# Cross-attention and quantised FFN, one core: every per-group stage placed anew, and the second quantisation's scale read from PSUM

## What is computed

```python
def act_quant(x):
    scale = 127.0 / jnp.clip(jnp.max(jnp.abs(x), axis=-1, keepdims=True), 1e-05)
    return jnp.clip(jnp.round(x * scale), -128, 127) / scale
...
q_in = x @ Wq + _lora(x, q_down, q_up, q_alpha)
k_in = org_ctx @ Wk + _lora(org_ctx, k_down, k_up, k_alpha)
v_in = org_ctx @ Wv + _lora(org_ctx, v_down, v_up, v_alpha)
out = _attention(q_in, k_in, v_in)
out_ipa = _attention(q_in, ipa_ctx @ Wk_ipa, ipa_ctx @ Wv_ipa)
out = out + IPA_SCALE * out_ipa
return out @ Wo + bo + _lora(out, o_down, o_up, o_alpha)
...
h = bit_linear(x, w1)
h = depthwise_conv1d(h.transpose(0, 2, 1), conv_w, conv_b)
h = h.transpose(0, 2, 1)
h = jax.nn.silu(h)
return bit_linear(h, w2)
...
x = x + _L0_xattn_ref(_layernorm(x, axis=-1), ctx_768, ...)
x = x + _L0_ffn_ref(_layernorm(x, axis=-1), ...)
```

## Time and profile before

| | us |
|---|---|
| median of 3 runs | 1633.49 (1632.47 to 1634.84) |
| profiled execution | 1633.91 |
| its span | 1631.8 |
| PE busy | 1458.5 (89%) |
| DVE busy | 1244.0 (76%) |
| ACT busy | 1188.6 (73%) |
| POOL busy | 730.8 (45%) |

### The profile page before, as it was taken

One profiled execution on the slowest core, in us unless ns is written; L12 is line 12 of the kernel. 1 busy time (PEld: TensorE's weight loads), 2 busy tenths in 40 slices (PEclk: granted clock), 3 DMA queues, 4 the chain that ended last, 5 costly groups with the idle time before them and its releaser, 6 DMA issues.

```text
span 1631.8 us, 33414 instructions
## 1 busy us (share of the span) xinstructions
PE 1458.5 (89%) x10732; PEld 1190.0 (73%) x10778; DVE 1244.0 (76%) x3029; ACT 1188.6 (73%) x3925; POOL 730.8 (45%) x1085
## 2 busy tenths in 40 slices
PE   7999998999999999999999899999989999998742
PEld 3778787777777777777787777777877777776521
DVE  4263697887878788777879878786888878786876
ACT  2477886968778686968778696877869687886721
POOL 0144444554544444554444445454454445445510
PEclk9999999999999999999999999999999999999965
DMA  7300101000000100000010100001010000000000
GB/s 192 119 29 15 30 15 43 2 27 28 27 28 14 41 14 28 14 27 28 14 41 14 34 7 27 28 19 35 14 41 13 28 14 27 28 1 27 1 14 13
DMA packets 41129, 47.14 MB, mean 29 GB/s; under 512 B 3008, under 2 KB 35200, under 8 KB 41088
## 3 DMA queue, kind: packets, MB, share of 16 engines
q1 hardware_dynamic: 40032, 45.82, 9.1%
q10 hardware_dynamic: 1056, 0.81, 0.2%
HBM read 36.13 MB, written 10.49 MB: 29 GB/s over the span
## 4 chain that ended last, share of the span: by engine, by line
PE 32%; issue 29%; POOL 17%; DVE 13%; ACT 8%; DMA 0%; POOLq 0%; DVEq 0%; ACTq 0%
POOL SM L1033 8%; PE PS L462 6%; POOL OTl L1065 5%; PE PS L424 5%; PE PS L523 4%; ACT SM L650 3%; PE PS L475 3%; PE PS L449 3%; PE PS L405 3%; PE PS L440 3%; POOL XRES L1072 2%; PE PS L414 2%; DVE GBS L869 1%; DVE HP L754 1%; PE PS L542 1%
## 5 line engine op out<-in xcount | busy, mean ns | idle before, releaser
L1033 POOL TENSOR_TENSOR SM<-SM,RC 128x496 f32<-128x496 f32 (+1 forms) x512 | 338.9, 683 | 673.8 <-DVE RC L804 673.8
L650 ACT ACTIVATE SM<-PS,MX 128x124 f32<-128x124 f32 x1024 | 359.2, 366 | 160.1 <-DVE SM L810 158.0
L462 PE MATMUL PS<-KT,QM 128*128 128x128 f32 x2048 | 279.3, 280 | 25.6 <-ACT SM L650 25.4
L462 PEld LDWEIGHTS PS<-KT,QM 128*128 128x128 f32 x2048 | 251.4, 193 | 37.9 <-ACT SM L650 37.2
L1065 POOL TENSOR_TENSOR OTl<-OF,OTh 128x256 fp32r<-128x256 f32 x256 | 210.4, 822 | 16.0 <-ACT OF L644 15.2
L650 ACT ACTIVATION_READ_ACCUMULATOR SM<-PS,MX 128x1 f32 x1024 | 211.3, 206 | 0.0
L449 PE MATMUL PS<-IDF,SM 128*128 128x128 f32 x1024 | 168.4, 287 | 35.6 <-POOL SM L1033 35.4
L642 ACT ACTIVATE OTh<-PS 128x256 fp32r<-128x256 f32 x256 | 100.2, 392 | 113.1 <-PE PS L440 111.8
L808 DVE TENSOR_REDUCE MX<-PS 128x4 f32<-128x496 f32 x256 | 170.0, 664 | 0.0
L440 PE MATMUL PS<-PT,V 128*64 128x128 f32 x2048 | 169.2, 286 | 0.0
L449 PEld LDWEIGHTS PS<-IDF,SM 128*128 128x128 f32 x1024 | 107.8, 141 | 81.8 <-POOL SM L1033 43.8
(11 more groups left out here) (140 smaller groups left out, 3663.0 us busy)
## 6 DMA issues: line engine op xcount, KB each, us to landing
XIN<-in_x SPq DMA_DIRECT2D x16, 512.0 KB, 3.5
XRES<-in_x SPq DMA_DIRECT2D x16, 512.0 KB, 3.5
out_y<-HP SPq DMA_DIRECT2D x16, 512.0 KB, 3.0
CRAW<-in_ctxT SPq DMA_DIRECT2D x16, 256.0 KB, 2.7
RRAW<-in_ctxT SPq DMA_DIRECT2D x32, 128.0 KB, 2.9
QM<-in_Wq SPq DMA_DIRECT2D x1, 1024.0 KB, 10.8
GBS<-in_Wo SPq DMA_DIRECT2D x1, 1024.0 KB, 21.7
k_ipa_columns<-HP SPq DMA_DIRECT2D x1, 1024.0 KB, 5.1
```

The lines of the kernel that those rows point to most:

```text
L462: m = mm(psS[:, h, :], QM[:, 2 * q + h // 2, h % 2, TOK * b:TOK * b + TOK], KT[:, 2 * q + h // 2, b, :], start=True, stop=True)
L650: m = act.activation(SM[s % 2][:, h, 0:ORG], psS[:, h, 0:ORG], ACT.Exp, bias=MX[s % 2][:, h:h + 1], accum_out=SU[s % 2][:, h:h + 1])
L1033: m = pool.tensor_tensor(part, part, RC[c % 2][:, 4 * i:4 * i + 4].unsqueeze(2).broadcast_to(shape), ALU.mult)
```

## The change

**All places are new.** The units of a quad now come in the order Q K Q K V V, with a list of halves for each quad instead of a common pattern. The hidden tiles take the offsets 0, 1, 3, 4, 6, 7, 9, 10 instead of 0, 1, 2, 4, 5, 6, 8, 9, so everything behind them starts a half later, and the transposes of the maxima and the second broadcast come closer behind the maxima: M_HMAX 28 to 29, M_HT 30 to 31, M_BC2 32 as before, M_Q2 33 as before. The two blocks of the second product move from 36 and 38 to 38 and 40. The two residual sums move from halves 4 and 7 to 6 and 7, the largest absolute value gets a half of its own (10) and the scales half 11. The split of the context is in half 7 on ScalarE and 8 on VectorE, ScalarE's copies of the transposed input in half 9 instead of 8. The context's DMAs are issued at half 5 instead of 7, those of the image tokens' values at the halves of the first V.

**Second quantisation.** VectorE multiplies all eight tiles, and reads the scale from psF in PSUM; the copy to BC on ScalarE and the two multiplies on GpSimd are gone. Four tiles are done in half 33, two in 34, two in 35 (Q2_PLACE); the rounding is the same.

**Buffers.** XN2 and Q1 lie in GBS instead of HP. **GpSimd** issues the chunk's attention work ahead of the other stages in each half.

```diff
-U_Q, U_K, U_V = (0, 3), (1, 4), (2, 5)
+U_Q, U_K, U_V = (0, 2), (1, 3), (4, 5)
...
-N_CIN = 7
-N_CSPLIT = 8
+N_CIN = 5
+N_CSPLIT = (7, 8)
 N_KI = 10
-N_Q, N_K, N_V = (10, 14), (11, 15), (13, 16)
-N_QUAD = (0, 8, 15, 23)
+N_Q = ((10, 17, 24, 31), (12, 20, 27, 34))
+N_K = ((11, 18, 26, 33), (13, 21, 28, 35))
+N_V = ((15, 22, 29, 36), (16, 23, 30, 37))
...
-M_X2 = (4, 7)
+M_X2 = (6, 7)
 M_STATS = 7
-M_POW, M_NORM = 9, 9
-M_QT, M_BC1 = 13, 14
+M_POW, M_NORM = 8, 9
+M_ABS, M_SCALE = 10, 11
+M_QT, M_BC1 = 12, 14
 M_F1 = 15
-M_TILE = (0, 1, 2, 4, 5, 6, 8, 9)
+M_TILE = (0, 1, 3, 4, 6, 7, 9, 10)
...
-M_HT, M_BC2 = M_HMAX + 2, M_HMAX + 4
-M_Q2 = M_HMAX + 5
-M_F2 = (M_HMAX + 8, M_HMAX + 10)
+M_HT, M_BC2 = M_HMAX + 2, M_HMAX + 3
+M_Q2 = M_HMAX + 4
+M_F2 = (M_HMAX + 9, M_HMAX + 11)
 M_COPY = M_Q2 + 2
-Q2_DVE = CT - CT // 4
+Q2_PLACE = (0, 0, 1, 2)
...
-        XN2 = h_rows[:, 6:8, :].rearrange("p a (b d) -> p (a b) d", d=DM)
-        Q1 = h_rows[:, 5, :].bitcast(BF16).rearrange("p (b d) -> p b d", d=DM)
+        gb_flat = GBS[:].rearrange("p i b t -> p (i b t)")
+        XN2 = gb_flat[:, 2 * T:4 * T].rearrange("p (b d) -> p b d", d=DM)
+        Q1 = gb_flat[:, T:2 * T].bitcast(BF16).rearrange("p (b d) -> p b d", d=DM)
...
-                if n == N_XT:
+                if n == N_XT + 1:
                     for k in range(2):
                         act.wait_ge(unit_full, g.count(UNITS, k + 1))
...
-                for j in range(CT):
-                    if n == M_Q2 + j // 4 and j % 4 < 3:
-                        dve.wait_ge(bc_done, g.count(2, 2))
-                        if j >= 4:
-                            dve.wait_ge(q2_done, g.count(CT, j - 3))
-                        dve.tensor_tensor(GB[j % 4].rearrange("p b t -> p (b t)"), HT[j], BC[:], ALU.mult).then_inc(q2_scaled[0], 1)
...
+                pairs = [k for k in range(CT // 2) if n == M_Q2 + Q2_PLACE[k]]
+                for j in (2 * k + i for k in pairs for i in range(2)):
+                    dve.wait_ge(bc_full, g.count(2, 2))
+                    if j >= 4:
+                        dve.wait_ge(q2_done, g.count(CT, j - 3))
+                    dve.tensor_tensor(GB[j % 4].rearrange("p b t -> p (b t)"), HT[j], psF, ALU.mult).then_inc(q2_scaled, 1)
...
             def steps(g, n):
+                attend(g, n)
+                attend_low(g, n)
                 if g.exists():
                     project(g, n + HALVES)
...
                 residual(g, n)
-                attend(g, n)
-                attend_low(g, n)
```

More of the change, by code:

```diff
@@ L255, in program @@
         hm_done, ht_full = sem("hm_done"), sem("ht_full")
-        q2_scaled = [sem(f"q2_scaled{i}") for i in range(2)]
+        q2_scaled = sem("q2_scaled")
         q2_done = sem("q2_done")
@@ L884, in finish @@
                     scales(g, 1, 2 * CLIP, 127.0, 1.0 / 254.0)
-                for j in range(CT):
-                    if n == M_Q2 + j // 4 and j % 4 < 3:
-                        dve.wait_ge(bc_done, g.count(2, 2))
-                        if j >= 4:
-                            dve.wait_ge(q2_done, g.count(CT, j - 3))
-                        dve.tensor_tensor(GB[j % 4].rearrange("p b t -> p (b t)"), HT[j], BC[:], ALU.mult).then_inc(q2_scaled[0], 1)
-                for j in range(CT):
-                    if n == M_Q2 + j // 4:
-                        if j % 4 == 0:
-                            dve.wait_ge(q2_scaled[0], g.count(Q2_DVE, 3 * (j // 4) + 2))
-                        if j % 4 == 2:
-                            dve.wait_ge(q2_scaled[0], g.count(Q2_DVE, 3 * (j // 4) + 3))
-                            dve.wait_ge(q2_scaled[1], g.count(CT - Q2_DVE, j // 4 + 1))
+                pairs = [k for k in range(CT // 2) if n == M_Q2 + Q2_PLACE[k]]
[4 more added lines that the diff above has]
+                    dve.tensor_tensor(GB[j % 4].rearrange("p b t -> p (b t)"), HT[j], psF, ALU.mult).then_inc(q2_scaled, 1)
+                for k in pairs:
+                    dve.wait_ge(q2_scaled, g.count(CT, 2 * k + 2))
+                    for j in range(2 * k, 2 * k + 2):
                         dve.tensor_scalar(Q2[j], GB[j % 4].rearrange("p b t -> p (b t)"), MAGIC, MAGIC,
@@ L1039, in finish @@
                     pool.tensor_tensor(RS[1][:], VE[1][:], HALF[:], ALU.pow).then_inc(ln2_rstd, 1)
-                for j in range(CT):
-                    if n == M_Q2 + j // 4 and j % 4 == 3:
-                        pool.wait_ge(bc_done, g.count(2, 2))
-                        if j >= 4:
-                            pool.wait_ge(q2_done, g.count(CT, j - 3))
-                        pool.tensor_tensor(GB[j % 4].rearrange("p b t -> p (b t)"), HT[j], BC[:], ALU.mult).then_inc(q2_scaled[1], 1)
             for n in range(EARLY_HALVES):
@@ L1068, in residual @@
             def residual(g, n):
-                if n in (16, 18, 20, 22) and g.exists():
-                    b = (n - 16) // 2
+                if n in (17, 19, 21, 23) and g.exists():
+                    b = (n - 17) // 2
                     pool.wait_ge(xres_in, g.count(16, 16))
```

50 lines of the change are left out of this document (23 added, 27 removed).

## The result

The changed kernel takes 1590.87 us (median of four runs, 1588.63 to 1592.11), the kernel before beside it 1633.92: a ratio of 0.9736, interval 0.9719 to 0.9753. The profiled execution took 1588.63, its span is 1586.8.

The account below looks back on a forecast made before the run. TensorE was taken as the bound, gaining only from its waits and clock. Loop -35, groups 0 and 1 +4, group 15 -6 and drain -6 give -43 us, so 1633.9 becomes 1591; range 1552 to 1626.

Parts of the forecast that it names:

- The quantisation: Second quantisation: 0.68 us a multiply, 7.6 on VectorE; the 3.1 us of waits in chunk 1 and the low clock go.
- What is late next: Six TensorE waits per loop period that the new order makes or keeps, sum 4.9 us, 4.6 after a deduction.
- the second block: Second product, half 8: TensorE waits 1.5 us for VectorE's sum of the first block, behind chunk 4's maxima.
- the tiles: Two pairs of hidden tiles in consecutive halves of one chunk wait for VectorE's multiply, 0.8 and 0.7 us a period.
- TensorE's work: TensorE's busy time in a loop period: the same matmuls are issued, so 86.4 us stays.
- Rival (c): Loop: waits only move, sum stays 6.3, clock still falls, period 93.7; 1626 us, or about 1631 without group 15's gain; 0.12.
- The start: Groups 0 and 1: 4 us more, from a Q unit ahead of the first scores (1.4) and group 1's new waits.
- Group 15: The last group before the drain: 7 us less in chunks 0 to 4, 1 more behind, so 6 less.
- The drain: The chain at the end: quantisations, BC copy and a filled VectorE wait save, tiles cost 1.2; together 6 us less.
- (a): Loop: VectorE comes on time, small delays do not add up, only 1.8 us of waits; period 88.3, 1556 us; chance 0.18.
- (b): Second quantisation becomes the bound, multiplies 1.17 us from start to start; period 94.9, 1651 us; 0.08 with lesser forms.
- (d): The main forecast, but the clock falls every second period after the 1.5 us wait: 10 more, 1601 us; 0.62 together.

Follow-up runs that it names:

- r3: The changed kernel with the second scale copied to BC and all eight multiplies on VectorE reading it from there; 1614.0 us.
- r4: The changed kernel with VectorE's sum of the second product's first block one half earlier; 1595.1 us.
- r7: r1 with ScalarE's two copies of the transposed input one half later, behind that chunk's exponentials; 1582.9 us.
- r1: The kernel before with only the quantisation from PSUM, all eight multiplies on VectorE, four tiles in each of two halves; 1584.5 us.
- r6: The changed kernel with the projection's units, and the context's transfers and split, in the order and halves of before; 1566.2 us.
- r5: The changed kernel with all its new places but the old second quantisation (copy to BC, two multiplies on GpSimd); 1629.1 us.

## Why the prediction was right, point by point

**The total** was 1591 and came out at 1590.9, and that is partly luck. The loop gave 43.3 instead of 35, the drain 2.2 instead of 6, and the start cost 6.7 instead of 4 (2.3 of it the first scores, which scatter by as much); by the spans it is 45.0 less, where the sum had 43.

**The quantisation** was right in every number: 0.68 a multiply, 0.60 from start to start, 3.8 for the first piece (884.29 to 888.0), no wait for GpSimd's probabilities, no low clock. That the 65 ns more for an operand in PSUM would not show held too. What the text left open is which part of it matters. r3 shows it in part: the wait for the copy is the most of it, and the operand's place matters by what GpSimd's work beside it no longer does, not by a price of its own.

**What is late next.** All six terms came, each in its place: 1.2 for the second block (predicted 1.5), 0.6 for the maxima (0.8), 0.6 for the K copy (0.4), 0.5 for BC (0.7; some 0.3 without the matmul that the trace lacks), 0.8 and 0.8 for the tiles (0.8 and 0.7). Their sum is 4.6, as predicted after the deduction. But they are not six independent costs: r4 shows that the second block's 1.2 can go and the period stay, since chunks 5 and 7 then wait for GpSimd and for BC.

**TensorE's work** was to stay 86.4. It is 85.8: the mis-sized term. The prediction had the better number at hand: its list of the sixteen chunks adds up to 85.3, which the sum did not use. The loop's 43.3 are 24 for the waits (13 x (6.45 - 4.6)), 9.3 for the clock (6 x 1.55) and 9 for less work (13 x 0.7), where the sum of 35 has none for the last. Scores behind a wait for the exponentials read 1.16 where others read 1.06 (r7's row above). Measured to the next instruction's start, the scores of r1 take 0.91 behind such a wait and 0.81 otherwise, in four chunks (1, 4, 5, 13) of each period; the transposes ahead of the wait take 0.65 to their end, and 0.49 to the next start where nothing waits. They are not slower: the four start within 0.38 in both cases, but the last one's end, which otherwise lies under the first scores, stands alone ahead of a wait, and the first scores behind it are 0.10 longer. In the changed kernel all sixteen chunks have 0.81 and 0.49. Such a wait therefore costs some 0.26 more than its idle time, 1.0 a period; the rest of the period takes 0.3 more than in r1, which stays unexplained. r6 has 86.5 again, so the smaller work belongs to the units' new halves, whose idle time more than takes it back.

**The reason for the gain** was half wrong. I read the light and heavy chunks as the place "where the order loses". r1 has them all and the same period as after; r5, without them but with the old quantisation, has 93.1. The imbalance made a late engine visible, it was not the cause, and the new halves of the units, taken alone, lose 1.2 a period (r6). Rival (c), that waits only move, was right for the places, though not for the kernel.

**The start** was to cost 4. Groups 0 and 1 cost 4.4 between them. The 1.4 for a Q unit ahead of the first scores cannot be seen in the scatter there; group 1, with 3.4, costs more than I gave it. r6 has both back.

**Group 15** was to give 6 and gave 6.1, by 6.3 in chunks 0 to 4 and 0.2 lost behind, where the prediction had 7 and 1.

**The drain** was to give 6 and gave 2.2. The two quantisations gave 2.4 and 0.8 (10.2 to 7.8 and 8.6 to 7.8 us from first multiply to last rounding), as predicted together. The copy to BC gave 0.6 in the last group (2.97 to 2.34 us from the last scale to the first multiply), not 0.8; filling VectorE's 3.1 us wait gave 0.65, not 2.4, since the second block runs at the lower clock level there and makes VectorE wait 2.39 itself (its 16 matmuls take 3.58 at a granted clock of 0.52; before they took 1.92 at 1.00). The prediction's sum for the drain has no term for the clock:

```profile
1520.13 0.88 DVE L818 SCALAR_TENSOR_TENSOR HP<-PS,AD,HP 128x256 f32<-128x256 f32 x2 [0.51 <-PE PS L525]
...
1524.68 0.88 DVE L818 SCALAR_TENSOR_TENSOR HP<-PS,AD,HP 128x256 f32<-128x256 f32 x2 [2.39 <-PE PS L525]
```

The tiles cost 0.1, not 1.2. And a term was missing: the maxima stand a half later, so from the last scores to the first multiply it is 10.05 instead of 7.76, 2.3 more.

**Small sums.** 4.4 + 1.6 + 0.8 is 6.8, not 6.9, and (c) with nothing from group 15 is 1632, not 1631; neither changes the forecast.

**Rivals.** (a) fell, the delays did add up. (b) fell with 689 ns as the longest multiply. (d) fell with the clock at 1.00: no wait of the loop was followed by the lower level.

## What to carry to other kernels

Before placing stages anew, find the engine whose lateness the waits express, and shorten or spread its work; here the cheaper quantisation gave 43 us and spreading it over one more half 14 (1.1 x 13), while of the five edits that took away a single wait of TensorE four got back nothing and one lost 20 us (r4's edit also delayed the chain that TensorE waits for next). As these runs suggest, a wait is worth removing only if the chain behind the next one also starts earlier. Undo a many-part change part by part even when the total is as predicted: the kernel with the units' old places and the quantisation spread (r10_spread, 1555.6 us) is 35 us faster than the change as made.
